# A four-layer gated transformer on one core: placing side work inside two attention streams and a feed-forward block

## Chip, cores and metric

The kernel runs on one core of one Trainium2 chip. The metric is device time in microseconds (us) of one launch. Times are given as the median of three runs; one further execution was recorded by the hardware profiler.

## What is computed

Input `x` is (4, 256, 256), the context is (4, 256, 64). Four layers follow one another, each of the form "x plus tanh(gate) times an attention of the normalised x, then x plus tanh(gate) times a feed-forward of the normalised x". Cut to what the change touches:

```python
# layer 1: attention with 32 query and 8 key heads, then a block with its own causal attention
x = x + tanh(g[1]) * grouped_attention(layernorm(x), ctx, ctx)      # "l1x"
attn = causal_attention(rmsnorm(h), Wq, Wk, Wv) @ Wo.T              # "l1f", h = layernorm(x)
mod = 0.1 * tanh(attn @ A)
gate = silu(h2 @ W_in.T + mod * (h2 @ A) @ B); out = h + gate * (h2 @ W_up.T) @ W_down.T
# layer 2: adjacency from two score vectors, then a block with quantised rows and ternary weights
x = x + tanh(g[2]) * (0.6 * sigmoid(si + sj + b) + 0.4 * layernorm(x))
h = layer_norm(gelu(silu(bitlinear(layernorm(x), w1, b1))), ln_g, ln_b)
x = x + tanh(f[2]) * bitlinear(h, w2, b2)
#   bitlinear: scale = 127 / max|row|; q = clip(round(row * scale)) / scale; q @ ternary(w).T + b
# layer 3: grouped attention, then a soft mixture of 16 experts with 128 slots each
x = x + tanh(g[3]) * (grouped_attention(layernorm(x), ctx, ctx) @ Wc.T + bc)   # "l3x"
mu_n = mu / max(sqrt(sum(mu * mu, axis=0)), 1e-12)                  # the slot norms
logits = einsum(l2norm(x_ln), mu_n); ...
```

## The kernel before

The program is one static stream of instructions for each engine; nothing is scheduled by a planner. The order is written by hand, as Python loops with conditions on a pair (slot, tile), and semaphores link the engines. The token rows stay in on-chip memory the whole time (`xs`, tiles of 128 rows by 256). Every batch has two such tiles.

In order of time the stages are:

- up to about 474 us: preparation of weights, layer 0's attention and its mixture of experts;
- 474 to 768 us: the first attention stream, called "A" in the code, which holds layer 1's two attentions for all four batches;
- 768 to 935 us: layer 1's feed-forward in two halves of 512 tokens, layer 2's adjacency, and the first half of layer 2's quantised block;
- 935 to 1105 us: the second attention stream, "C", which is layer 3's attention, with the quantised block's second half in between;
- from there on: the soft mixture.

**A stream.** `attention(stream)` loops over slots `sl`, from -3, and over tiles `k` from 0 to 7. A slot is one group of heads of one batch. Stream A has 16 slots of l1x (four to a batch, so batch 0 has slots 0 to 3, and `LAST["l1x", b]` is 3, 7, 11, 15), then 8 of l1f. Stream C has 8 slots of l3x, two to a batch. At tile k TensorE makes scores for slot `sl` with the keys as rows (`by_key`, L1064, read by ScalarE's exponential) and for slot `sl + 2` with the queries as rows (`by_query`, L1016, of which VectorE takes the largest value, L2120). GpSimd splits these maxima into bf16 parts, a DMA lays them out again, and TensorE turns them (`turn_maxima`, L1027). Queries and keys of slot `sl + 3` are turned at tiles 3, 5, 6 and 7 (L948, L969), `weighted` (L1084) multiplies with the values, and once in each slot `rows_again` (L1100, rows of `otr`) turns an output back into rows.

**The batch's way from l1x to l1f** lies between these steps. When the last l1x slot of batch b, slot e, is through, VectorE adds and normalises the rows (`between`), GpSimd applies weights (`rows_in`), and TensorE turns the two results (`turn_rows`, L611 on `tmp` and `qr`), then projects to queries and keys (`queries_and_keys`, L1117, two steps for each of two halves) and values (`values`). All the turnings and these projections, and rows_again, share two banks of the product memory, `left0` and `left1`, in an order that `bank_uses` sorts from the same (slot, tile) pairs; a step can take its bank once the step two places before it has been copied out by ScalarE or VectorE. Before, TensorE does `turn_rows` at (e+2, 6) and (e+2, 7), the first projections at (e+3, 0) and (e+3, 1), the second ones at (e+3, 5) and for batches 0 and 1 (e+3, 6), the values at (e+4, 0) and (e+4, 1).

**The slot norms.** `slot_products` (L1280) sums the squares of `mu` by 64 products of one column, VectorE takes the reciprocal roots (`slot_norms`, 19 operations on 128x16), `turn_slot_parts` turns them, `spread_slots` spreads them over partitions into banks 6 and 7, and VectorE scales `mu` (`scale_slots`). They stand in the first half of the feed-forward, between its gate groups (`gate_and_up`, L1253 and L1255).

**The quantised block**, half h. ScalarE normalises and centres (L1702, L1709), quantises, and TensorE multiplies (`l2_up`). ScalarE makes silu and gelu, VectorE the layer norm (`l2_shift`, L2372) and the largest value of each row (L2375). `l2_square` (L1736) sums squares on ScalarE. VectorE then scales and rounds the hidden rows in one pass, by adding and later subtracting a large constant (`l2_round_hidden`, L2384), ScalarE makes bf16 of them (`l2_second_quantised`, L1742), TensorE turns and multiplies (`l2_last`: `turn_hidden` L1337, `l2_down` L1346), VectorE adds the rows (L2393) and takes their statistics. For h = 1, `l2_last` stands at (-1, 7) of stream C, ahead of slot 0. The third banks of both halves are in `L2_BANKS`. ScalarE's `norm` (L1570) and GpSimd's parts of the queries and keys (L2575, L2578) of batches 2 and 3 need these rows.

The two loops on which the order in TensorE's stream hangs:

```python
for sl in range(-3, S_ + (1 if stream == "A" else 2)):
    for k in range(8):
        if inside(sl) and k < tiles_of(groups[sl][0]):
            by_key(sl, k)
...
        if inside(sl + 2) and k < tiles_of(groups[sl + 2][0]):
            by_query(sl + 2, k)
```

## Time and profile before

| what | value |
|---|---|
| runs | 1325.32, 1324.08, 1322.42 us; median 1324.08 |
| profiled execution | 1326.74 us |
| its span, first to last instruction | 1325.0 us |
| granted clock of TensorE, mean | 0.916 of full |
| TensorE, matrix products (PE) | 1057.4 us busy, 80% |
| TensorE, weight loads (PEld) | 672.3 us |
| VectorE (DVE) | 740.0 us, 56% |
| ScalarE (ACT) | 525.4 us, 40% |
| GpSimd (POOL) | 328.2 us, 25% |

"Busy" is time in which an engine runs an instruction. In a row of the timeline, the first number is the start in us, the second the duration, the bracket the idle time before it and the instruction that ended the wait. `L1100` is a line of the kernel. A name with q, such as DVEq, is the engine's own queue, a semaphore instruction without work. The rows quoted in a later section are of this one execution.

### The profile page before, as it was taken

The numbers are of one execution on the slowest core, as the hardware profiler recorded it, in microseconds if no ns is written. First come the engines' busy times: TensorE is split into PE (matmuls) and PEld (weight loads), VectorE is DVE, ScalarE is ACT, GpSimd is POOL, SyncE is SP. The second block draws the span as 40 slices with busy tenths as digits, with TensorE's granted clock in tenths as the row PEclk, the third lists the DMA queues.
The fourth block names the chain that finished last, engine by engine and source line by source line (L and its number), as shares of the span: only waits on it lengthen the run. The fifth ranks groups of instructions, "written<-read, shape, count | busy, mean of one in ns | idle before, by whom it ended". The sixth has DMA issues, their size and how long they took to land.

```text
span 1325.0 us, 19053 instructions
## 1 busy us (share of the span) xinstructions
PE 1057.4 (80%) x6622; PEld 672.3 (51%) x6625; DVE 740.0 (56%) x1684; ACT 525.4 (40%) x883; POOL 328.2 (25%) x626
## 2 busy tenths in 40 slices
PE   4245999999999678778798889984252888899997
PEld 2124888888888533233355645533232443475565
DVE  3654444544454646685655512457777765676644
...
DMA packets 62441, 32.06 MB, mean 24 GB/s; under 512 B 47104, under 2 KB 61072, under 8 KB 62112
## 3 DMA queue, kind: packets, MB, share of 16 engines
...
q14 instruction: 29, 0.24, 0.1%
...
## 4 chain that ended last, share of the span: by engine, by line
PE 69%; DVE 20%; ACT 4%; issue 4%; POOL 1%; SPq 0%; DMA 0%; POOLq 0%; DVEq 0%; ACTq 0%; PEldq 0%
PE bank L692 15%; PE bank L708 7%; PE bank L800 4%; PE bank L1084 3%; DVE mx L2120 3%; PE bank L915 2%; PE bank L883 2%; PE bank L1016 2%; PE bank L1270 2%; PE bank L845 2%; PE bank L1253 2%; PE bank L1064 2%; PE bank L1255 2%; PE bank L1117 2%; PE bank L1100 1%
## 5 line engine op out<-in xcount | busy, mean ns | idle before, releaser
L2120 DVE TENSOR_REDUCE mx<-bank 128x2 f32<-128x512 f32 (+1 forms) x176 | 118.1, 689 | 88.6 <-PE bank L1016 44.8
L1594 ACT ACTIVATE prob<-bank 128x512 f32<-128x512 f32 x176 | 102.7, 597 | 100.1 <-PE bank L1064 78.3
L1433 ACT ACTIVATE hhi<-hh 128x512 fp32r<-128x512 f32 x72 | 45.5, 632 | 153.1 <-DVE hh L1957 140.5
L1953 DVE TENSOR_TENSOR hu<-bank,sg 128x512 f32<-128x512 f32 x64 | 44.3, 692 | 101.6 <-PE bank L692 101.6
L692 PE MATMUL bank<-xh,wh 128*128 128x512 f32 x288 | 91.5, 398 | 0.7 <-POOL wl L2539 0.7
L692 PE MATMUL bank<-xh,wl 128*128 128x512 f32 x288 | 90.5, 395 | 0.0
L692 PE MATMUL bank<-xlo,wh 128*128 128x512 f32 x288 | 90.1, 394 | 0.0
L1945 DVE TENSOR_TENSOR hlo<-hh,hhi 128x512 fp32r<-128x512 f32 x72 | 57.1, 793 | 50.6 <-ACT hhi L1433 50.6
L2539 POOL TENSOR_TENSOR wl<-wraw,wh 128x512 fp32r<-128x512 f32 x72 | 80.4, 1117 | 13.0 <-POOL wh L2536 13.0
L1472 ACT ACTIVATE sg<-bank 128x512 f32<-128x512 f32 x72 | 43.1, 598 | 64.8 <-PE bank L692 64.8
L692 PEld LDWEIGHTS bank<-xh,wh 128*128 128x128 f32 x288 | 54.4, 189 | 14.6 <-POOL wl L2539 1.6
L692 PEld LDWEIGHTS bank<-xlo,wh 128*128 128x128 f32 x288 | 54.3, 189 | 13.4
L692 PEld LDWEIGHTS bank<-xh,wl 128*128 128x128 f32 x288 | 54.4, 189 | 12.4
L800 PE MATMUL bank<-mun,xT 128*128 128x512 f32 x128 | 59.2, 607 | 1.2 <-ACT xw L1433 1.1
L708 PE MATMUL bank<-hhi,wh 128*128 128x512 f32 x144 | 56.8, 394 | 0.9 <-DVE hlo L1945 0.9
L708 PE MATMUL bank<-hhi,wl 128*128 128x512 f32 x144 | 56.9, 395 | 0.0
L708 PE MATMUL bank<-hlo,wh 128*128 128x512 f32 x144 | 56.1, 390 | 0.0
L1016 PE MATMUL bank<-kTx,qT 48*128 48x256 bf16 x256 | 51.4, 308 | 3.7 <-DVE kTx L2084 3.1
L1064 PE MATMUL bank<-qT,kTx 51*128 51x512 bf16 x128 | 51.9, 421 | 2.6 <-ACT prob L1594 2.5
L2120 DVE TENSOR_REDUCE mxc<-bank 128x2 f32<-128x512 f32 x64 | 42.6, 687 | 20.2 <-PE bank L1016 19.1
L1594 ACT ACTIVATE probc<-bank 128x512 f32<-128x512 f32 x64 | 37.5, 596 | 40.0 <-PE bank L1064 39.4
L1337 PE MATMUL bank<-identb,q 128*128 128x128 bf16 x64 | 7.8, 298 | 56.7 <-ACT q L1742 56.7
...
## 6 DMA issues: line engine op xcount, KB each, us to landing
...
```

Source lines behind the costliest of these rows:

```text
L692: last = mm(bank[4 + (n + m) % 4][:, :], w[k % 2][:, m, cc * P:(cc + 1) * P], v[:, cc, tok], start=j == 0 and cc == 0, stop=j == 2 and cc ...
L708: last = mm(bank[2 * m + h][:, :], w[k % 2][:, 2, m * P:(m + 1) * P], v[h][:, :], start=False, stop=last_pair and j == 2, skip_group_check ...
L800: last = mm(bank[n % 2][:, :], xT3[b % 2][:, cc, i * P:(i + 1) * P], mun[:, cc, ch * 512:(ch + 1) * 512], start=cc == 0, stop=cc == 1)
L1016: last = mm(to[:, f * N:(f + 1) * N], t.qT[rows, s % 4, u, i * P:(i + 1) * P], key_operand(L, b, s, 8 * g + 2 * j + f, rows, slice(0, N)), ...
L1064: last = mm(to[:, :], key_operand(L, b, s, 8 * g + 2 * j, rows, slice(ti * P, (ti + 1) * P)), t.qT[rows, s % 4, u:u + 2, :], start=True, s ...
L1433: return act.activation(dst, src, ACT.Copy, scale=scale)
L1472: act.activation(sg[k % 2][:, :], bank[4 + n % 4][:, :], ACT.Silu).then_inc(once("gate_used"), 1)
L1594: act.activation(t.prob[k][:, :], bank[3 + n % 2][:, :], ACT.Exp).then_inc(S("probs"), 1)
L1945: tt(hlo[k % 2][:, :], hh[k % 2][:, :], hhi[k % 2][:, :].bitcast(F32), ALU.subtract)\
L1953: tt(hu[k % 2][:, :], bank[4 + (n + 1) % 4][:, :], sg[k % 2][:, :], ALU.mult).then_inc(once("up_used"), 1)
L2120: V.reduce_max(out_, bank[n % 3][:, :].rearrange("p (h t) -> p h t", h=heads), AX, negate=True)\
L2539: G.tensor_tensor(low[:, cols, :], wraw[k][:, cols, :], high[:, cols, :].bitcast(F32), ALU.subtract)\
```

## The change

Four things are placed differently.

1. *First stream.* A table `BETWEEN` now gives the places of the turnings and projections. For batches 0 and 1 the turnings go from (e+2, 6) and (e+2, 7) to (e+3, 0) and (e+3, 1), the first projections from (e+3, 0) and (e+3, 1) to (e+3, 5) and (e+3, 6), the second ones to (e+4, 0) and (e+4, 1), the values to (e+4, 5) and (e+4, 6). For batch 2 the projections go to (e+4, 0/1) and (e+5, 0/1), the values to (e+6, 0/1). Batch 3 is as it was. The copies on ScalarE and VectorE that empty the banks move with them, as `_out` says.
2. *Slot norms.* They leave the first half of the feed-forward and stand in the second, from its gate group 1 on; all four spreads use bank 7. The turned parts' copy on ScalarE moves along.
3. *Rounding pass.* ScalarE does it as an Identity with scale and bias (`l2_round_hidden`), before each tile's quantising, for both halves. VectorE only signals that the scales are ready.
4. *Last products of the second half.* `l2_last(1)` and all that feeds it from the squares on move from (-1, 7) to (0, 7) of stream C, on banks 0 to 2, and ScalarE's norms of batches 2 and 3 to (1, 0) and (2, 0).

```diff
@@ -49,6 +49,28 @@
+Between = namedtuple("Between", "t0 t0_out t1 t1_out qk0 qk0_out qk1 qk1_out v v_out")
+
+
+def between_at(b):
+
+    e = LAST["l1x", b]
+    if b == B - 1:
+        return Between(t0=(e + 2, 6), t0_out=(e + 2, 7), t1=(e + 2, 7), t1_out=(e + 3, 0), qk0=((e + 3, 0), (e + 3, 1)),
+                       qk0_out=(e + 3, 1), qk1=((e + 3, 5), (e + 3, 5)), qk1_out=(e + 3, 5), v=((e + 4, 0), (e + 4, 1)),
+                       v_out=(e + 4, 1))
+    if b == B - 2:
+        return Between(t0=(e + 3, 0), t0_out=(e + 3, 1), t1=(e + 3, 1), t1_out=(e + 3, 2), qk0=((e + 4, 0), (e + 4, 1)),
+                       qk0_out=(e + 4, 1), qk1=((e + 5, 0), (e + 5, 1)), qk1_out=(e + 5, 2), v=((e + 6, 0), (e + 6, 1)),
+                       v_out=(e + 6, 1))
+    return Between(t0=(e + 3, 0), t0_out=(e + 3, 1), t1=(e + 3, 1), t1_out=(e + 3, 2), qk0=((e + 3, 5), (e + 3, 6)),
+                   qk0_out=(e + 3, 7), qk1=((e + 4, 0), (e + 4, 1)), qk1_out=(e + 4, 2), v=((e + 4, 5), (e + 4, 6)),
+                   v_out=(e + 4, 7))
+
+
+BETWEEN = [between_at(b) for b in range(B)]
@@ -74,9 +96,9 @@
-            e = LAST["l1x", b]
-            at += [(e + 2, 6, 4, ("t", b, 0)), (e + 2, 7, 4, ("t", b, 1)), (e + 3, 0, 4, ("qk", b, 0)),
-                   (e + 3, 5, 4, ("qk", b, 1)), (e + 4, 0, 4, ("v", b))]
+            w = BETWEEN[b]
+            at += [(*w.t0, 4, ("t", b, 0)), (*w.t1, 4, ("t", b, 1)), (*w.qk0[0], 4, ("qk", b, 0)),
+                   (*w.qk1[0], 4, ("qk", b, 1)), (*w.v[0], 4, ("v", b))]
...
+L2_LATE_BANKS = ((4, 5, 6), (0, 1, 2))
...
-            b = L2_BANKS[h][n % 3]
+            b = (L2_BANKS if n < Q2T_USE[0] else L2_LATE_BANKS)[h][n % 3]
...
@@ -991,6 +1014,8 @@
+                    if stream == "C" and n == 24:
+                        pe.wait_ge(S("l2_rows"), 2 * T0)
...
@@ -1033,7 +1058,7 @@
                     if stream == "C" and n == 0:
-                        pe.wait_ge(S("l2_rows"), 2 * T0)
+                        pe.wait_ge(S("l2_pre"), 16)
...
@@ -1170,21 +1195,20 @@
                             if stream == "A":
-                                e = LAST["l1x", b]
-                                if (sl, k) == (e + 2, 6):
+                                w = BETWEEN[b]
+                                if (sl, k) == w.t0:
                                     turn_rows(b, 0)
-                                if (sl, k) == (e + 2, 7):
+                                if (sl, k) == w.t1:
                                     turn_rows(b, 1)
-                                if sl == e + 3 and k < 2:
-                                    queries_and_keys(b, 0, k)
-                                if (sl, k) == (e + 3, 5):
-                                    queries_and_keys(b, 1, 0)
-                                    if b >= 2:
-                                        queries_and_keys(b, 1, 1)
-                                if (sl, k) == (e + 3, 6) and b < 2:
-                                    queries_and_keys(b, 1, 1)
-                                if sl == e + 4 and k < 2:
-                                    values(b, k)
+                                for cc in range(DC):
+                                    if (sl, k) == w.qk0[cc]:
+                                        queries_and_keys(b, 0, cc)
+                                for cc in range(DC):
+                                    if (sl, k) == w.qk1[cc]:
+                                        queries_and_keys(b, 1, cc)
+                                for i in range(NT):
+                                    if (sl, k) == w.v[i]:
+                                        values(b, i)
                             else:
                                 e = LAST["l3x", b]
...
                                     l2_up(1, i)
-                            if (sl, k) == (-1, 7):
+                            if (sl, k) == (0, 7):
...
-                if ch >= 2:
-                    pe.wait_ge(S("mu_normed"), ch - 1)
+                else:
+                    pe.wait_ge(S("mu_normed"), ch)
-                    last = mm(bank[6 + ch % 2][:, e % 4 * SS:(e % 4 + 1) * SS], sel[:, e, :], cmT[:, :], start=True, stop=True)
+                    last = mm(bank[7][:, e % 4 * SS:(e % 4 + 1) * SS], sel[:, e, :], cmT[:, :], start=True, stop=True)
-                if n >= 3:
+                if h == 1 and Q2T_USE[0] <= n < Q2T_USE[0] + 3:
+                    pe.wait_ge(S("maxed"), 24)
+                elif n >= 3:
-                    pe.wait_ge(S("mu_normed"), 4)
+                    pe.wait_ge(S("cT2"), 2)
...
@@ -1360,34 +1386,31 @@
 
             for f in range(F1 // P):
                 gate_and_up(0, f)
-                if f == 1:
-                    slot_products()
-                if f == 3:
-                    turn_slot_parts()
-                if f == 5:
-                    spread_slots(0)
-                    spread_slots(1)
-                if f == 6:
-                    spread_slots(2)
-                if f == 7:
-                    spread_slots(3)
             gate_and_up(1, 0)
             for i in range(T0):
                 down(0, i)
             for f in range(1, F1 // P):
                 gate_and_up(1, f)
+                if f == 1:
+                    slot_products()
                 if f == 4:
                     turn_inputs(0)
                 if f == 5:
+                    turn_slot_parts()
                     l2_up(0, 0)
                     l2_up(0, 1)
                 if f == 6:
+                    spread_slots(0)
                     l2_up(0, 2)
                     l2_up(0, 3)
+            spread_slots(1)
             for i in range(T0):
                 down(1, i)
+                if i < 2:
+                    spread_slots(2 + i)
             l2_last(0)
             pe.wait_ge(S("ffn_out"), 2 * T0)
+            pe.wait_ge(S("mu_normed"), 4)
 
             attention("C")
...
@@ -1613,10 +1636,9 @@
-                        if stream == "C" and k == 0 and inside(sl + 4) and groups[sl + 4][1] >= 2 and groups[sl + 4][2] == 0:
-                            if groups[sl + 4][1] == 2:
-                                act.wait_ge(S("ln_x"), 2)
-                            norm(groups[sl + 4][1])
+                        if stream == "C" and (sl, k) in ((1, 0), (2, 0)):
+                            act.wait_ge(S("ln_x"), 2)
+                            norm(sl + 1)
...
@@ -1651,10 +1673,11 @@
                             if (sl, k) == (-2, 6):
                                 for i in range(T0):
                                     l2_gelu(1, i)
-                            if (sl, k) == (-1, 7):
+                            if (sl, k) == (0, 7):
                                 for i in range(T0):
                                     l2_square(1, i)
                                 for i in range(T0):
+                                    l2_round_hidden(1, i)
                                     l2_second_quantised(1, i)
                                 for i in range(T0):
...
+            def l2_round_hidden(h, i):
+
+                act.wait_ge(S("l2_r2"), h + 1)
+                act.activation(h2[:, i, :], h2[:, i, :], ACT.Identity, bias=l2v[:, 57:58], scale=l2v[:, 52 + i:53 + i])\
+                    .then_inc(S("l2_r3"), 1)
+
-                act.wait_ge(S("l2_r2"), T0 * h + i + 1)
+                act.wait_ge(S("l2_r3"), T0 * h + i + 1)
...
-                if f == 4:
-                    act.wait_ge(S("mu_partsT_ps"), 1)
-                    copy(cmT[:, :], bankb[7][0:96, 0:P]).then_inc(S("mu_partsT"), 1)
+            act.wait_ge(S("mu_partsT_ps"), 1)
+            copy(cmT[:, :], bankb[7][0:96, 0:P]).then_inc(S("mu_partsT"), 1)
...
@@ -2226,6 +2255,7 @@
                                     l2_stats(1, i)
                                 l2_norm2(1)
                                 l2_shift(1)
+                            if (sl, k) == (0, 7):
                                 l2_round_hidden(1)
                                 l2_add(1)
                                 stats_of(step, 0.25, range(T0, 2 * T0))
...
-                for i in tiles:
-                    ts(h2[:, i, :], h2[:, i, :], l2v[:, 52 + i:53 + i], ROUND, ALU.mult, ALU.add).then_inc(S("l2_r2"), 1)
+                dve.sem_inc(S("l2_r2"), 1)
...
@@ -2396,16 +2425,11 @@
 
             for f in range(F1 // P):
                 hidden(0, f)
-                if f == 2:
-                    slot_norms()
                 if f == 4:
                     l2_scores(0)
                     l2_scores(1)
-                if f >= 5:
-                    scale_slots(f - 5)
             dve.wait_ge(once("late_rows"), len(rowsF) * 16)
             hidden(1, 0)
-            scale_slots(3)
             for i in tiles:
                 add_down(0, i)
             l2_norm(0)
@@ -2415,19 +2439,24 @@
             l2_round_inputs(0)
             hidden(1, 3)
             hidden(1, 4)
+            slot_norms()
             l2_pre(0, 0)
             l2_pre(0, 1)
             hidden(1, 5)
             l2_pre(0, 2)
             l2_pre(0, 3)
             hidden(1, 6)
+            scale_slots(0)
             hidden(1, 7)
+            scale_slots(1)
             l2_stats(0, 0)
             l2_stats(0, 1)
             add_down(1, 0)
+            scale_slots(2)
             l2_stats(0, 2)
             l2_stats(0, 3)
             add_down(1, 1)
+            scale_slots(3)
             l2_norm2(0)
```

The first place is TensorE's order in slots 5 and 6 of stream A, for batch 0 (e = 3). `kstx` is a key operand, `tmp` and `qr` are the two results to be turned, `wqkvT` the projection's weights. Before:

```order
L969 MATMUL bank<-identb,kstx 128x128 x8
L1016 MATMUL bank<-kTx,qT 128x256 x2
L1064 MATMUL bank<-qT,kTx 128x512
L611 MATMUL bank<-ident,tmp 128x128 x4
L1016 MATMUL bank<-kTx,qT 128x256 x2
L1064 MATMUL bank<-qT,kTx 128x512
L969 MATMUL bank<-identb,kstx 128x128 x8
L611 MATMUL bank<-ident,qr 128x128 x4
L1016 MATMUL bank<-kTx,qT 128x256 x2
L1064 MATMUL bank<-qT,kTx 128x512
L1117 MATMUL bank<-wqkvT,xT 128x512
```

and after the change:

```order
L992 MATMUL bank<-identb,kstx 128x128 x8
L1041 MATMUL bank<-kTx,qT 128x256 x2
L1089 MATMUL bank<-qT,kTx 128x512
L1041 MATMUL bank<-kTx,qT 128x256 x2
L1089 MATMUL bank<-qT,kTx 128x512
L992 MATMUL bank<-identb,kstx 128x128 x8
L1041 MATMUL bank<-kTx,qT 128x256 x2
L1089 MATMUL bank<-qT,kTx 128x512
L634 MATMUL bank<-ident,tmp 128x128 x4
```

with the second turning behind it, after the products with the values:

```order
L1109 MATMUL bank<-prob_173,vstx 32x512
L634 MATMUL bank<-ident,qr 128x128 x4
L1041 MATMUL bank<-kTx,qT 128x256 x2
L1089 MATMUL bank<-qT,kTx 128x512
```

The turnings of `tmp` and `qr` no longer stand ahead of the second key turning and right behind it, but after it and in the next slot; the two projection steps, formerly behind the second turning (the first of them is the last row of the first piece), follow at that slot's tiles 5 and 6.

The second place is ScalarE's order around the second half's squares (`q_225,l2v<-h_224`, and `h_224` is the hidden rows). Before, at the end of the slots ahead of slot 0 (`probc` are the exponentials of slot 0):

```order
L1433 ACTIVATE qTc<-bank 96x1024
L1736 ACTIVATE q_225,l2v<-h_224 128x1024 x4
L1742 ACTIVATE q_225<-h_224,l2v 128x1024 x4
L1433 ACTIVATE q2T<-bank 128x8x128 x4
L1594 ACT_TABLE_LOAD
L1594 ACTIVATE probc_197<-bank 128x512
L1570 ACTIVATE xnc<-xs,nmx,rsx 128x256 x2
L1594 ACTIVATE probc_198<-bank 128x512
L1594 ACTIVATE probc_199<-bank 128x512
L1594 ACTIVATE probc_200<-bank 128x512
L1433 ACTIVATE mTc<-bank 24x256
```

and after the change, where slot 0's exponentials come first:

```order
L1617 ACTIVATE probc_200<-bank 128x512
L1456 ACTIVATE mTc<-bank 24x256
L1617 ACTIVATE probc_201<-bank 128x512
L1456 ACTIVATE qTc<-bank 96x1024
L1617 ACTIVATE probc_202<-bank 128x512
L1617 ACTIVATE probc_203<-bank 128x512
L1617 ACTIVATE probc_204<-bank 128x512
L1759 ACTIVATE q_225,l2v<-h_224 128x1024 x4
L1764 ACTIVATE h_224<-h_224,l2v 128x1024
L1771 ACTIVATE q_225<-h_224,l2v 128x1024
L1764 ACTIVATE h_224<-h_224,l2v 128x1024
L1771 ACTIVATE q_225<-h_224,l2v 128x1024
```

The squares now stand behind slot 0's eight exponentials, and each quantising is preceded by a rounding of the same rows.

## Rows read from the trace of the kernel before

**Rows 1.** Busy time by stage: us, PE, PEld, DVE, ACT, POOL (instructions), PEclk, DMA share, GB/s
```profile
474.00:768.00 294.00, 238.32 (x2448) 118.57 (x2448) 182.38 (x410) 155.88 (x275) 115.88 (x309) 0.87 0.01 4
...
935.00:1105.00 170.00, 99.14 (x993) 54.19 (x994) 122.40 (x290) 87.06 (x134) 31.56 (x81) 0.75 0.01 2
```

**Rows 2.** Timeline, TensorE, slots 5 and 6: start, us, instruction [idle before <-releaser]
```profile
544.01 0.63 PE L611 MATMUL bank<-ident,tmp 128*128 128x128 f32 x4 [2.23 <-DVEq L2143]
...
546.99 1.03 PE L969 MATMUL bank<-identb,kstx 128*128 128x128 bf16 x8 [2.02 <-DVE kTx L2084]
...
550.89 2.04 PE L1117 MATMUL bank<-wqkvT,xT 128*128 128x512 f32 x2 [1.47 <-DVE kTx L2084]
...
561.50 1.12 PE L1117 MATMUL bank<-wqkvT,xT 128*128 128x512 f32 x2
```

**Rows 3.** Timeline, TensorE: the output turnings of slots 5 to 8
```profile
538.95 0.63 PE L1100 MATMUL bank<-ident,otr 128*128 128x128 f32 x4 [0.18 <-ACT mT L1433]
...
559.62 0.63 PE L1100 MATMUL bank<-ident,otr 128*128 128x128 f32 x4 [0.73 <-ACT mT L1433]
...
570.65 0.66 PE L1100 MATMUL bank<-ident,otr 128*128 128x128 f32 x4
...
577.97 0.63 PE L1100 MATMUL bank<-ident,otr 128*128 128x128 f32 x4 [0.18 <-ACT mT L1433]
```

**Rows 4.** Timeline, TensorE: the output turnings of slots 13 to 16
```profile
634.86 0.67 PE L1100 MATMUL bank<-ident,otr 128*128 128x128 f32 x4 [0.18 <-ACT mT L1433]
...
660.18 0.66 PE L1100 MATMUL bank<-ident,otr 128*128 128x128 f32 x4
...
677.83 0.66 PE L1100 MATMUL bank<-ident,otr 128*128 128x128 f32 x4
...
688.35 0.61 PE L1100 MATMUL bank<-ident,otr 128*128 128x128 f32 x4
```

**Rows 5.** Timeline, TensorE, the feed-forward block
```profile
787.10 1.98 PE L1253 MATMUL bank<-hT,winT 128*128 128x512 f32 x4
...
791.78 10.23 PE L1280 MATMUL bank<-ones,mu 128*128 128x1 f32 x64
...
869.36 3.78 PE L1253 MATMUL bank<-hT,winT 128*128 128x512 f32 x4 [3.16 <-DVE gu L2265]
```

**Rows 6.** Timeline, ScalarE and VectorE, the quantised block's first half
```profile
917.86 2.08 ACT L1702 ACTIVATE xn<-xs,l2v 128x256 f32<-128x256 f32 x4 [17.45 <-DVEq L2311]
...
935.39 2.74 DVE L2384 TENSOR_SCALAR h<-h,l2v 128x1024 f32<-128x1024 f32 x4
...
941.75 1.70 ACT L1709 ACTIVATE xn<-xs,l2v 128x256 f32<-128x256 f32 x4 [1.30 <-DVEq L2324]
```

**Rows 7.** Timeline, ScalarE and VectorE, the second half's last chain
```profile
1000.85 1.06 ACT L1736 ACTIVATE q<-h 128x1024 bf16<-128x1024 f32 x1 [18.43 <-DVE h L2372]
...
1004.43 4.42 DVE L2375 TENSOR_REDUCE l2v<-h 128x4 f32<-128x4096 f32 x1
...
1013.01 4.27 ACT L1742 ACTIVATE q<-h,l2v 128x1024 bf16<-128x1024 f32 x4 [7.42 <-DVE h L2384]
...
1024.59 0.48 DVE L2393 SCALAR_TENSOR_TENSOR xs<-bank,l2v,xs 128x256 f32<-128x256 f32 x1 [0.81 <-PE bank L1346]
```

**Rows 8.** Timeline, from the norm to the turning of slot 2's maxima
```profile
1029.59 1.09 ACT L1570 ACTIVATE xnc<-xs,nmx,rsx 128x256 f32<-128x256 f32 x2 [3.44 <-DVEq L2232]
...
1030.82 0.40 POOL L2575 CAST qstc<-xnc 128x256 bf16<-128x256 f32 x1 [43.46 <-ACT xnc L1570]
...
1031.22 0.61 PE L1064 MATMUL bank<-qTc,kTc 99*128 99x512 bf16 x1 [4.09 <-ACT probc L1594]
...
1034.57 0.43 POOL L2578 TENSOR_TENSOR kstc<-leftc,kstc 128x128 bf16<-128x128 f32 x1
...
1038.46 0.20 POOL L2646 CAST mstc<-mxc 128x16 bf16<-128x16 f32 x1 [3.47 <-DVE mxc L2120]
...
1039.84 0.28 PE L1027 MATMUL bank<-identb,mstc 128*24 128x128 bf16 x2
```

22 lines of the change are left out of this document (11 added, 11 removed), and 1 row of the table STAGES.

## Prediction

> **What bounds the kernel now.** I read the granted clock and the busy time by stage first, then the order of TensorE's waits in the first attention stream, then the chain through the quantised block. In the first stream (474 to 768 us) TensorE is busy 238 of 294 us, at 0.87 of its full clock; in the second stream with the quantised block's second half (935 to 1105 us) 99 of 170 us, at 0.75 [rows 1]. TensorE is the bound, with holes; every term below is a hole that closes, moves or opens. I call one turn of the slot loop a slot; the marks for a slot's length are the four turnings back of an output (`rows_again`), one set in each slot.
>
> **The first stream, batches 0 and 1.** In slot 5 TensorE waits 2.23 us for the first turning's input, 2.02 us at the key turning and 1.47 us before the first projection, 5.7 us in all; after that two projection steps take 2.04 us where the same two take 1.12 us later [rows 2]. A quiet slot takes 7.3 us (570.65 to 577.97), the two disturbed ones 31.7 us together (538.95 to 570.65) [rows 3]. Two quiet slots and the moved work (two turnings at 0.63, six projection groups at about 1.12: 7.9 us) make 22.5; 9.2 us are loss.
>
> The key turning waits for VectorE's copy of the keys before it, and VectorE doesn't get there sooner when TensorE does. So the first two waits (4.3 us) become one wait of about 4.3 us at the key turning, before which the turning of `tmp` no longer fits: it costs 0.6 us that was hidden. What goes is the third wait (1.5) and the double price of the projections (1.8, twice 2.04 less 1.12), since they now stand in the middle of slot 6, after TensorE has worked again. 1.5 + 1.8 - 0.6 = 2.7 us for batch 0, the same for batch 1, whose stretch repeats it. Bounds: 0.9 (the clock stays low as long as before) and 4.9 (of the 9.2 only the 4.3 stay).
>
> **Batch 2** meets the masked attention's slots. Slots 13 to 15 take 25.3 and 17.65 us between marks, the next 10.5 us [rows 4]; 43.0 less two such slots (21.0) less the work (7.9) is 14.1 us of loss. The wait for the key copy with its slow stretch stays (about 5 us by batch 0's rows), and I add 1.6 us for two buffers that are now taken while their copy is under way (a wait of the kind of 0.7 to 0.9 us at the mark of slot 6 [rows 3]). 14.1 - 5.0 - 1.6 = 7.5 us. The values, moved to slot 17, run beside VectorE's next chain of small operations and cost TensorE nothing; without that cover they'd cost 2.2. Bounds: 3 (waits reappear at each moved step) and 9. Batch 3 stays in place.
>
> **The slot norms.** The 64 one-column products take 10.2 us [rows 5] in either place, and so do the turning and the four spreads. They leave the first half of the feed-forward and come back in the second, behind the group that stands before VectorE's two norms. There TensorE waits 3.16 us for VectorE and then runs four products in 3.78 us that otherwise take 1.98 [rows 5]. With 10.2 us of work put in front, VectorE is ready before TensorE asks: 3.2 + 1.8 = 5.0 us gained. The small operations on VectorE move into its waits between gate groups, which are 4.7 us apart (787.10 to 791.78 [rows 5]); uncovered they'd cost up to 4. Bounds: 3 and 6.
>
> **The rounding pass, first half.** It leaves VectorE (four tiles in 2.74 us, 0.69 each) and goes to ScalarE, where the quantising that follows takes 4.27 us for four [rows 6, 7]. It has a scale operand more; four such of 256 columns take 2.08 against 1.70 us, 0.1 us each [rows 6]. So a rounding is 1.17, a pair 2.24, four pairs about 9.0 us, strictly one after the other. ScalarE starts when VectorE's scales are there (935.4), ends at 944.4, then centres the other half (1.7 us): 946.1 instead of 943.4, so 2.7 us lost. Bounds 2.2 and 3.3.
> The Trainium skill speaks against this move (VectorE: DVE Perf Modes, the perf-mode tier table: a float32 tensor_scalar within SBUF runs at two results a cycle; ScalarE: Activation LUTs, What ACT_TABLE_LOAD costs: one element a cycle whatever the function, 280 ns and 0.833 ns per column with a pointer bias, 93 ns for each further pointer). The trace agrees in kind, 0.69 against 1.07 us. By the page's figures, as an estimate, a pair is 2.36 us, and the sum below would be 0.8 us worse over both halves.
>
> **The last products of the second half** move behind slot 0 of the second stream. I count from the end of VectorE's largest-value reduction (1004.43 + 4.42 = 1008.85 [rows 7]) to the turning of slot 2's maxima (1039.84 [rows 8]): 31.0 us now. Then, in series:
> - rest of slot 0 (tiles 3 to 7), since its third tile waits for VectorE's maxima: 7.0. A whole turn of eight tiles, from 1031.22 to 1039.84, takes 8.6 [rows 8]: ceiling that, floor five eighths of it, 5.4; the middle, since TensorE has idled before.
> - the four squares, until now beside VectorE, but placed behind the slot's exponentials: 4 x 1.2 = 4.8 (1.06 and the read of the sum [rows 7]).
> - VectorE's scales: 1013.01 - 1008.85 - 0.7 = 3.4 [rows 7].
> - four pairs on ScalarE: 9.0.
> - copies, turnings, products and the row additions: 1025.07 - 1017.3 = 7.8 [rows 7].
> - statistics of the new rows: 1029.59 - 1025.07 = 4.5 [rows 7, 8].
> - ScalarE's norm: 1.1 [rows 8].
> - GpSimd, whose order is unchanged: the query and key parts of batch 2 (1030.82 to 1035.00) 4.2, and only behind them slot 2's maxima (1038.46 to 1039.84) 1.4 [rows 8]. Before, those parts were ready 3.5 us ahead of the maxima.
>
> With 0.2 between them that is 43.4 us, 12.4 more. While GpSimd works TensorE waits some 8 us, and before (4.09 us [rows 8]) it ran at the lower level for a few us after such a wait; I add 1.0. Total 13.4 lost, bounds 10 and 18. What comes back for it, TensorE's slot 0 beside VectorE's normalisation, is in this count already: only its first three tiles.
>
> **Sum:** -2.7 - 2.7 - 7.5 - 5.0 + 2.7 + 13.4 = -1.8 us. The profiled execution took 1326.74 us (span 1325.0); the median of the runs is 1324.08, 2.7 below it. Taken off the median: **1322.3 us**. About 2.6 us (0.2%) is what a measurement can tell from no change, so this is a small gain or none.
>
> **The rivals.**
> 1. *The balance tips to slower: VectorE's backlog keeps the first stream.* Place: the key turning at the end of slots 5, 9 and 13. If the moved turnings find VectorE still behind, each later take of the two turning buffers waits for a copy, and the lower clock lasts as before. For it: TensorE's waits there name VectorE's key copy. Against it: VectorE has caught up by the third wait. The three batches then give 0.9 + 0.9 + 3.0 in place of 12.9: +6.3, 1330 us. It decides from a gain under 8.5 us in the first stream. Chance 0.22.
> 2. *The clock stays high.* If the spread work keeps TensorE fuller, the slow stretches (3.5 us of the 9.2 for each of batches 0 and 1, as much for batch 2) go as well, and batch 0 and 1 give 4.9 each, batch 2 9: with the quantised block at its lower bound (10 and 2.2) the sum is -11.6, 1312.5 us; with the block as counted -7.7, 1316. The Trainium skill (TensorE: Matmul & The Clock Gate, the part on the HAM clock gate) says that the throttled state is the default and activity releases it; that is this rival's rule. Against it: 4.3 us of idle stays. Chance 0.24.
> 3. *The quantised block's chain is longer than counted* (its second wait reaches the transfers of the maxima and the slots after): 18 in place of 13.4 and 3.3 for 2.7: +3.4, 1327.5. Chance 0.10.
> 4. *The late products don't hold the second stream* (GpSimd's parts fit, as before, in front of the maxima): 5 us less, -6.8, 1317. Chance 0.06.
>
> **How the numbers follow.** My forecast, the sum within about 3.5 us (1318.8 to 1325.8), has 0.38. Of it 0.26 lies within 0.2% and 0.12 below. Slower: rival 1 whole (0.22) and most of rival 3 (0.08). Faster: 0.12, rival 2 (0.24) and rival 4 (0.05). That makes 0.41 faster, 0.29 same, 0.30 slower. The range takes rivals 1 and 2: 1313 to 1331; in it are all cases but the outer ends of both.
>
> **What would show it.** In the new profile: marks of slots 5 to 7 some 3 us closer, of slots 13 to 15 some 7 closer or more, with one wait of about 4 us at the key turning; no wait of 3 us before the fourth gate group of the second half; eight ScalarE passes over the hidden rows in about 9 us, twice; TensorE idle for about 8 us ahead of the turning of slot 2's maxima, with GpSimd as the releaser. The prediction is wrong if the second stream reaches that turning less than 9 us late against the end of the reduction, or if the first stream shortens by less than 8 or more than 17 us.

## The result, and the profile after

The changed kernel takes 1333.22 us, median of five runs (1331.97 to 1338.64), against 1324.32 us of the kernel before, also of five (1322.42 to 1330.24). The ratio is 1.0068, with a 95% interval of 1.004 to 1.0096: 5 to 13 us slower. The forecast was 1322.3 us in a range of 1313 to 1331. Sign and range are both missed.

The profiled execution took 1331.97 us. From its page:

```profile
span 1330.2 us, 19059 instructions
## 1 busy us (share of the span) xinstructions
PE 1058.5 (80%) x6625; PEld 672.2 (51%) x6625; DVE 733.1 (55%) x1677; ACT 534.9 (40%) x891; POOL 329.0 (25%) x626
```

The same stretches of time as in [rows 1], start and end, length, PE, PEld, DVE, ACT, POOL (instructions), granted clock, DMA share, GB/s:

```profile
474.00:768.00 294.00, 242.43 (x2473) 120.79 (x2472) 184.57 (x432) 157.80 (x279) 118.59 (x305) 0.89 0.04 15
...
935.00:1105.00 170.00, 98.67 (x957) 51.00 (x955) 107.20 (x241) 84.11 (x128) 31.65 (x81) 0.74 0.01 2
```

The stages are no longer in the same places, so I cut both profiles at marks instead: the first and last output turning of the first stream (line 1100 before, 1125 after), the end of the feed-forward's last down product, the start of the quantised block's last product of the first half, the last turning of maxima in the second stream, and the end. The runs of the experiments are cut at the same marks in the tables further down. All are us of one profiled execution for each kernel.

| profile | first stream | feed-forward | first half | second stream | rest |
|---|---|---|---|---|---|
| before | 263.9 | 142.9 | 40.7 | 142.2 | 232.1 |
| changed | 256.6 | 136.9 | 43.6 | 158.7 | 233.0 |
| difference | -7.2 | -6.0 | +3.0 | +16.5 | +0.9 |
| forecast | -12.9 | -5.0 | +2.7 | +13.4 | 0 |

The differences make +7.1; the profiled execution of the change also began 1.9 us sooner ahead of these stages, where nothing was changed. Against the forecast's -1.8, the first stream is 5.7 us short, the second 3.1 too long, the first half 0.3 and the rest 0.9; the feed-forward gives back 1.0. The two profiled executions are only 5.2 us apart and the medians 8.9, so 3.7 us of the loss are not in this table; the runs of single parts below come closer to it.

**First stream, batch 0.** TensorE's timeline of the changed kernel in slots 5 to 8 (start, duration, instruction, idle before it and its releaser):

```profile
537.08 0.63 PE L1125 MATMUL bank<-ident,otr 128*128 128x128 f32 x4 [0.18 <-ACT mT L1456]
...
542.06 0.62 PE L992 MATMUL bank<-identb,kstx 128*128 128x128 bf16 x8 [1.83 <-DVEq L2172]
...
545.21 1.09 PE L634 MATMUL bank<-ident,tmp 128*128 128x128 f32 x4 [2.21 <-DVE kTx L2113]
548.03 0.37 PE L1041 MATMUL bank<-kTx,qT 48*128 48x256 bf16 x1 [1.73 <-DVE kTx L2113]
...
553.66 0.61 PE L971 MATMUL bank<-identb,qst 128*128 128x128 bf16 x8 [1.25 <-ACT hT L1456]
...
554.53 0.66 PE L1125 MATMUL bank<-ident,otr 128*128 128x128 f32 x4
...
556.44 1.12 PE L1142 MATMUL bank<-wqkvT,xT 128*128 128x512 f32 x2
...
565.32 0.61 PE L971 MATMUL bank<-identb,qst 128*128 128x128 bf16 x8 [1.53 <-DVE qkf L2113]
...
566.18 0.66 PE L1125 MATMUL bank<-ident,otr 128*128 128x128 f32 x4
...
575.38 0.63 PE L1125 MATMUL bank<-ident,otr 128*128 128x128 f32 x4 [0.41 <-ACT mT L1456]
...
585.08 1.11 PE L1125 MATMUL bank<-ident,otr 128*128 128x128 f32 x4
```

The marks of slots 5 and 9 are 48.0 us apart (585.08 less 537.08), and so were those of the kernel before (586.96, from the same view, less 538.95 [rows 3]). The kernel before waited three times in slot 5, 2.23, 2.02 and 1.47 us, 5.7 in all [rows 2]. The changed one waits three times too, 1.83, 2.21 and 1.73 us, 5.8 in all, for the same three things: VectorE's work on the slot's output, its copy of the first keys and its copy of the second keys. Only the step that waits is another: the third wait stood ahead of the projection and now stands ahead of a scores product (`kTx,qT`), which needs the same copy. VectorE's two key copies, before and then changed:

```profile
546.26 0.68 DVE L2084 COPY kTx<-bank 128x1024 bf16<-128x1024 bf16 x1
...
550.06 0.68 DVE L2084 COPY kTx<-bank 128x1024 bf16<-128x1024 bf16 x1
```

```profile
544.39 0.68 DVE L2113 COPY kTx<-bank 128x1024 bf16<-128x1024 bf16 x1
...
547.10 0.68 DVE L2113 COPY kTx<-bank 128x1024 bf16<-128x1024 bf16 x1
```

Counted from the mark of slot 5 the first copy starts at 7.3 us in both, the second at 11.1 before and 10.0 after. On top of that, two old steps (the next query turnings) now wait 1.25 and 1.53 us, because a moved step holds the turning buffer (releasers `hT` and `qkf`, the copies of the moved steps); before, this stretch had two waits of 0.73 and 0.93 us (the second from the same view). The projections are at 1.12 us as forecast, but the turning of `tmp` takes 1.09 in place of 0.63. So slot 5 shortens by 3.2 us, and 0.6, 1.9 and 0.7 come back in slots 6, 7 and 8. Slot 7 holds the two value steps now (2.2 us of work that slot 6 had before), but slot 6 didn't get shorter for their leaving: the 2.6 us by which slots 5 and 6 shorten together are little more than this work. At the end of slot 8 TensorE is at its lower level (1.11 us for a turning of an output, 0.63 at a quiet mark).

**Batch 2.** The marks of slots 13, 14, 15 and 18:

```profile
632.59 1.11 PE L1125 MATMUL bank<-ident,otr 128*128 128x128 f32 x4
...
651.24 0.66 PE L1125 MATMUL bank<-ident,otr 128*128 128x128 f32 x4
...
664.17 0.66 PE L1125 MATMUL bank<-ident,otr 128*128 128x128 f32 x4
...
707.72 0.61 PE L1125 MATMUL bank<-ident,otr 128*128 128x128 f32 x4
```

From 632.59 to 707.72 are 75.1 us, before 634.86 to 716.88, 82.0 us (the first mark stands in [rows 4], the last is from the same view): 6.9 gained. In the ten profiles with batch 2's new places this stretch takes 75.0 to 75.3 us, in the five with all old places 82.0 to 82.1.

**The feed-forward.** Behind the one-column products, before and then changed, with the changed kernel's gate group 4 of the second half (counted from 0) at the end:

```profile
801.87 3.76 PE L1253 MATMUL bank<-hT,winT 128*128 128x512 f32 x4
```

```profile
833.93 9.95 PE L1304 MATMUL bank<-ones,mu 128*128 128x1 f32 x64
843.73 3.76 PE L1277 MATMUL bank<-hT,winT 128*128 128x512 f32 x4
...
855.41 1.98 PE L1277 MATMUL bank<-hT,winT 128*128 128x512 f32 x4
```

No gate group waits any more, and group 4, which took 3.78 us behind its wait [rows 5], takes 1.98. The 3.76 us behind the one-column products stood there before the change too and moved along with them.

**The second half's chain**, ScalarE, VectorE, GpSimd and TensorE:

```profile
992.27 4.42 DVE L2405 TENSOR_REDUCE l2v<-h 128x4 f32<-128x4096 f32 x1
...
1008.10 0.17 DVE L2410 TENSOR_SCALAR ve<-l2v 128x4 f32<-128x4 f32 x1 [3.11 <-ACT q L1759]
...
1003.82 1.05 ACT L1759 ACTIVATE q<-h 128x1024 bf16<-128x1024 f32 x1
...
1011.48 1.24 ACT L1764 ACTIVATE h<-h,l2v 128x1024 f32<-128x1024 f32 x1 [3.41 <-DVEq L2413]
1012.75 1.15 ACT L1771 ACTIVATE q<-h,l2v 128x1024 bf16<-128x1024 f32 x1
...
1019.68 1.15 ACT L1771 ACTIVATE q<-h,l2v 128x1024 bf16<-128x1024 f32 x1
...
1033.81 1.09 ACT L1593 ACTIVATE xnc<-xs,nmx,rsx 128x256 f32<-128x256 f32 x2 [4.19 <-DVEq L2262]
...
1035.04 0.40 POOL L2604 CAST qstc<-xnc 128x256 bf16<-128x256 f32 x1 [59.83 <-ACT xnc L1593]
...
1039.46 0.20 POOL L2675 CAST mstc<-mxc 128x16 bf16<-128x16 f32 x1 [0.23 <-POOL kstc L2607]
...
997.47 0.61 PE L1041 MATMUL bank<-kTc,qTc 96*128 96x256 bf16 x2 [20.78 <-DVE mxc L2149]
...
1040.61 0.39 PE L1052 MATMUL bank<-identb,mstc 128*24 128x128 bf16 x2 [9.04 <-POOLq L2679]
1040.93 0.61 PE L1041 MATMUL bank<-kTc,qTc 96*128 96x256 bf16 x2
...
1051.65 0.28 PE L1052 MATMUL bank<-identb,mstc 128*24 128x128 bf16 x2
```

TensorE waits 20.8 us for VectorE's normalisation, runs the rest of slot 0, waits for the pairs on ScalarE, and waits 9.04 us more ahead of the turning of slot 2's maxima (1040.61).

### The profile page after: what moved, and what is told of

Read it like the earlier page. It is cut to its first block, busy times and chain, and to the rows that moved or that the text cites. A ratio compares the mean times of both kernels' runs of the same rounds, so it can differ in the third digit from the quotient of the medians.

```text
span 1330.2 us, 19059 instructions
## 1 busy us (share of the span) xinstructions
PE 1058.5 (80%) x6625; PEld 672.2 (51%) x6625; DVE 733.1 (55%) x1677; ACT 534.9 (40%) x891; POOL 329.0 (25%) x626
## 4 chain that ended last, share of the span: by engine, by line
PE 69%; DVE 19%; ACT 5%; issue 4%; POOL 1%; SPq 0%; DMA 0%; POOLq 0%; DVEq 0%; ACTq 0%; PEldq 0%
PE bank L715 15%; PE bank L731 7%; PE bank L823 4%; PE bank L1109 3%; DVE mx L2149 3%; PE bank L938 2%; PE bank L1277 2%; PE bank L1041 2%; PE bank L906 2%; PE bank L1294 2%; PE bank L868 2%; PE bank L1279 2%; PE bank L1089 2%; PE bank L1142 1%; PE bank L922 1%
## 5 line engine op out<-in xcount | busy, mean ns | idle before, releaser
L715 PEld LDWEIGHTS bank<-xlo,wh 128*128 128x128 f32 x288 | 54.3, 189 | 13.4
L715 PEld LDWEIGHTS bank<-xh,wl 128*128 128x128 f32 x288 | 54.4, 189 | 12.4
L2565 POOL CAST wh<-wraw 128x512 fp32r<-128x512 f32 x72 | 37.7, 523 | 58.8 <-PE bank L715 30.1
```

The costliest lines, as they stand in the source:

```text
L715: last = mm(bank[4 + (n + m) % 4][:, :], w[k % 2][:, m, cc * P:(cc + 1) * P], v[:, cc, tok], start=j == 0 and cc == 0, stop=j == 2 and cc ...
```

## The experiments

Each kernel is compared with the kernel before on the same chip, as a ratio with a 95% interval. The runs were made in four groups on three chips, so I compare kernels of different groups by these ratios, not by their medians. A time in us that I give for a ratio is the ratio times 1325.

**One part alone.** Each kernel is the one before with one of the four parts of the diff, otherwise unchanged. Where the rounding stays on VectorE, `l2_round_hidden` is the loop of `ts(...)` over four tiles as before; where the late products stay, `l2_last(1)` and what feeds it stand at (-1, 7).

> The kernel before, with only the first stream's new table of places. Theory A (the parts add as the two profiles show them: the stretch from the first output turning to the last gets 7.2 us shorter, none of it from batches 0 and 1, 6.8 from batch 2): 7 us faster than before, about 1317; marks of slots 5 to 9 as far apart as before (48 us). Theory B (the prediction's terms were right, and something else in the whole change took the gain of batches 0 and 1 away): 12.9 us faster, slots 5 to 9 in about 45 us.

> The kernel before, with only the slot norms in the feed-forward's second half. Theory A: the 3.2 us wait of TensorE before the fourth gate group of the second half and part of the slow matrix products behind it go, 5 to 6 us faster (1318 to 1319). Theory B (the gain was borrowed from another moved part, as the earlier arrival at the feed-forward): 2 us or less.

> The kernel before, with only the rounding pass on ScalarE, in both halves, the last products where they were. Theory A: 2.8 us lost in the first half (read from the two profiles) and 5.0 in the second, where nothing stands between the pairs and the turnings: 7 to 8 us slower (about 1332). Theory B (a pair on ScalarE overlaps VectorE's work): 5.4 or less, 2.7 a half as predicted.

> The kernel before, with only the last products of the second half moved behind slot 0 of the second stream, rounding still on VectorE. Theory A (chain through squares, scales, products, statistics and GpSimd's parts stands in series behind slot 0): 10 to 12 us slower (1334 to 1336), with TensorE idle for about 9 us ahead of the turning of slot 2's maxima. Theory B (the late place costs only with the rounding on ScalarE): within 4 us of before.

| run | median us | ratio | interval | first stream | feed-forward | first half | second stream |
|---|---|---|---|---|---|---|---|
| stream only | 1321.78 | 0.9968 | 0.9949 to 0.9988 | 257.4 | 143.1 | 40.7 | 145.1 |
| norms only | 1319.76 | 0.9951 | 0.9932 to 0.9969 | 264.0 | 136.9 | 40.3 | 144.6 |
| rounding only | 1334.27 | 1.007 | 1.0045 to 1.0095 | 264.0 | 142.9 | 43.7 | 148.7 |
| late products only | 1333.89 | 1.0079 | 1.0049 to 1.0109 | 260.0 | 142.9 | 40.7 | 153.7 |

By the ratios that is -4.2, -6.5, +9.3 and +10.5 us: +9.1 together, the change as measured is +9.0. The stream and the norms gain, the rounding pass and the late products each lose more than either gain. Each of these four carries 2.5 to 4 us of uncertainty to either side. Against the forecast (-12.9, -5.0, and by its terms +6.6 for the rounding and +9.5 for the late products) the first stream misses by 8.7 us, more than the other three together. I had expected 7 us of gain for the stream and 7 to 8 us of loss for the rounding. (In the rounding run the view merges the last two products of the first half into one row; the mark is the start of the last one, 952.10.)

The rounding pass costs 3.0 us in the first half and 6.5 in the second stream. Its profile in the second half, ScalarE:

```profile
1013.84 1.24 ACT L1767 ACTIVATE h<-h,l2v 128x1024 f32<-128x1024 f32 x1 [6.69 <-DVEq L2416]
...
1022.05 1.15 ACT L1774 ACTIVATE q<-h,l2v 128x1024 bf16<-128x1024 f32 x1
1023.10 1.92 ACT L1458 ACTIVATE q2T<-bank 128x1024 bf16<-128x1024 bf16 x2
```

The four pairs take 9.3 us here, against 5.1 for VectorE's four passes with ScalarE one behind (1012.22, where the first pass starts, to 1017.28 [rows 7]). Then the copies of the turned rows stand behind all four pairs on ScalarE (1023.10), and TensorE stays longer at its lower level in the turnings and products that follow (granted clock 0.65 between 1024 and 1032 us, against 0.78 between 1018 and 1025 before): from the first pair (1013.84) to TensorE's next product of slot 0 (1032.21 in the same view) are 18.4 us, before, from 1012.22 to 1025.13, 12.9.

The table shows something else. The second stream takes 142.2 us before, and 145.1 and 144.6 where only earlier stages were changed; the first stream 260.0 us where it wasn't touched at all (late products only). That led to the next question.

**Parts put together, and batches apart.** The stream and the norms together; batches 0 and 1 alone; batch 2 with the norms. In the table of places the batches left out got back the tuple that stands for the old code:

```diff
+    if b in (2,):
+        return Between(t0=(e + 2, 6), t0_out=(e + 2, 7), t1=(e + 2, 7), t1_out=(e + 3, 0), qk0=((e + 3, 0), (e + 3, 1)),
+                       qk0_out=(e + 3, 1), qk1=((e + 3, 5), (e + 3, 6 if b < 2 else 5)), qk1_out=..., v=((e + 4, 0), (e + 4, 1)), ...)
```

> The changed kernel with its rounding pass back on VectorE and its last products back ahead of slot 0, so the first stream's table and the slot norms alone. Theory A (the two gains of the single runs, 4 and 6 us, stand beside one another, since one closes before the other begins): 10 to 11 us faster than before, about 1315. Theory B (the earlier start of each later stage is eaten by longer stretches of the lower clock in the second stream, where each single run took 2 to 3 us more than before): 8 us or less in the profile, with the last turning of maxima over 144 us after the first half's last product.

> The kernel before with the new places for batches 0 and 1 only. Theory A (VectorE's copies are late by the same amount wherever the turnings stand, and the waits only move to them): no change beyond the noise; marks of slots 5 to 9 and of 9 to 13 as far apart as before, 48.0 and 47.9 us within 0.5. Theory B (the profile of the whole change hid a gain that its later marks lost to another batch): 5.4 us faster, 45 us for each four slots.

> Batch 2's new places and the slot norms; batches 0 and 1 as before. Theory A (batches 0 and 1 lose about what their own run lost, 7 us, whatever stands around them): 7 us faster than the stream and the norms together, about 1309. Theory B (batches 0 and 1 change nothing by themselves; what their own run lost is stretches at the lower clock that come with the time of arrival, so losses of single parts don't add): as fast as the stream and the norms together within 2 us, about 1315; slots 5 to 9 and 9 to 13 in 48 us each as before, slots 13 to 18 in some 59 in place of 63.7.

| run | median us | ratio | interval | first stream | feed-forward | second stream |
|---|---|---|---|---|---|---|
| stream and norms | 1315.89 | 0.9918 | 0.9896 to 0.9939 | 260.1 | 140.2 | 144.6 |
| batches 0 and 1 only | 1333.75 | 1.0061 | 1.0038 to 1.0084 | 266.8 | 146.4 | 142.4 |
| batch 2 and norms | 1314.15 | 0.9926 | 0.9905 to 0.9947 | 253.5 | 140.1 | 142.7 |

Batches 0 and 1 alone make the kernel 8 us slower, where I had expected no change, and yet taking them out of "stream and norms" gains nothing that the intervals can tell: theory B of the third run. Batch 2 and the norms gain 3.3 us more than the norms alone, give or take some 4. In the run of batches 0 and 1 the marks of slots 5, 9 and 13 are 48.0 and 47.5 us apart, as far as before, so its profile shows no loss where the moved steps stand. It is further on, in steps that were not moved: slots 13 to 17, 66.3 us in place of 63.7, behind the same waits of 2.52, 1.62 and 1.46 us (66.3 again in the second profile with these places, shown below), and the entry of the feed-forward block. At this entry TensorE waits 2.52 us in both kernels. In the one before, the turnings behind it and the next products:

```profile
770.33 1.97 PE L1224 MATMUL bank<-ident,at_f 128*128 128x128 f32 x16 [2.52 <-POOLq L481]
772.23 3.61 PE L1229 MATMUL bank<-hT,am 128*16 128x512 f32 x8
```

and with batches 0 and 1 moved:

```profile
771.53 3.68 PE L1249 MATMUL bank<-ident,at_f 128*128 128x128 f32 x16 [2.52 <-POOLq L507]
775.14 4.50 PE L1254 MATMUL bank<-hT,am 128*16 128x512 f32 x8
```

The same wait, the same instructions, 1.97 and 3.61 us against 3.68 and 4.50: TensorE ran them at its lower level (granted clock 0.66 of full between 770 and 780 us, and 1.00 in the profile before). The profiled execution as a whole is 5.1 us longer than that of the kernel before; what makes the rest of the 8 us stays open. Fifteen of the seventeen profiles have this wait unfilled, 2.51 or 2.52 us long: in twelve the turnings take 1.97 us, in three 2.37 to 3.68. There is one profile for each kernel, so they can't tell whether the edit decides this or the single execution. With the old places of batch 0 its four slots took 45.4 to 48.0 us in seven profiles, with the new ones 48.0 to 52.2 in ten, so the new places of batch 0 gain nothing and on the whole cost something. Batch 1's four slots took 47.6 to 48.0 us with the old places and 47.5 to 48.3 with the new ones.

**The lower level tested by filling waits.** If TensorE has products to do in the wait, no level should be lost. The first wait tried is the one at the entry of the feed-forward:

```diff
             attention("A")
+            keep_clock(6, 10)
             pe.wait_ge(S("at_done"), 2 * B)
```

`keep_clock(k, n)` is a helper of the kernel: n products of 128x512 into bank k, whose values nobody reads.

> The run with batch 2's places and the norms, with ten more matrix products (128x512, bf16, into a bank that is free) in TensorE's wait of 2.5 us at the entry of the feed-forward block. Theory A (what the wait costs beyond itself is the lower clock behind it, which some runs show and others don't): the sixteen turnings behind the wait take 2.0 us in each profile, and the median falls by 0 to 2.5 us. Theory B (the clock has nothing to do with the wait): the products cost their own time, up to 2 us slower.

> The run with the new places of batches 0 and 1 only, with ten more matrix products (128x512, bf16, into a bank that is free) in TensorE's wait of 2.5 us at the entry of the feed-forward block. Theory A (2.6 of the 7 us that run lost are the lower clock at that entry): 2 to 3 us faster than that run, about 1331, with the sixteen turnings there in 2.0 us in place of 3.7. Theory B (the loss sits elsewhere): 1333 to 1334.

Measured: with batch 2 and the norms 1313.52 us (0.9917, 0.9896 to 0.9937), against 1314.15 (0.9926) without; with batches 0 and 1 alone 1331.22 us (1.0043, 1.0029 to 1.0057), against 1333.75 (1.0061) on another chip. The entry of the latter:

```profile
772.06 2.10 PE L652 MATMUL bank<-mask_q,identb 128*128 128x512 bf16 x9 [1.24 <-DVEq L2176]
774.00 1.91 PE L1249 MATMUL bank<-ident,at_f 128*128 128x128 f32 x16
775.84 3.61 PE L1254 MATMUL bank<-hT,am 128*16 128x512 f32 x8
```

The turnings take 1.91 us and the products 3.61, and so they do in the other filled kernel. The filling products start 1.24 us into the wait and end 0.7 us after it would have ended, so from the last output turning to the first gate group are 15.9 us, against 17.9 unfilled and 15.3 in the kernel before: 2.0 us back. That the filling did it isn't shown: twelve of fifteen unfilled profiles have the upper level there too, and the ratios differ by 1.2 and 2.4 us, with intervals that overlap.

The other wait is the one of 9.04 us in the late arrangement. The products go into the bank that the turning writes next:

```diff
+                    if stream == "C" and s == 2:
+                        r, full, _ = of_use(stream, ("m", s))
+                        pe.wait_ge(S(f"left{r % 2}"), r // 2)
+                        for _ in range(24):
+                            mm(full[:, :], identb[:, :], mask_q[:, :, :], start=True, stop=True, skip_group_check=True)
                     pe.wait_ge(S("max_parts"), s + 1)
```

> The changed kernel, with 24 more matrix products (128x512, bf16, into the bank that the turning is about to write) in TensorE's wait of 9.0 us ahead of the turning of slot 2's maxima. Theory A (3.2 us of the late products' loss over the prediction is the lower clock behind that wait): slot 2's to slot 3's turning of maxima takes 8.8 us in place of 11.0; 2 to 4 us faster than the change, about 1330. Theory B (these slots are longer for their new order of work): still 11.0 us between the two turnings, no change in the median or some tenths slower.

> The changed kernel, with 44 more matrix products (128x512, bf16, 0.22 us each at the full clock, 9.5 in all) in the wait of 9.0 us ahead of the turning of slot 2's maxima. Theory A (the slow slots behind the wait are the lower clock, and the 24 products failed since 3.85 us of idleness were left): 8.8 us from slot 2's to slot 3's turning in place of 11.0, 1 to 2 us faster than the change if the products end with the wait. Theory B (the slots are long by their work): 11.0 us stay, and the products that overrun make it up to 1 us slower.

With 24 products the median is 1333.55 us (1.0077, 1.0054 to 1.0099), with 44 it is 1330.82 (1.0045, 1.0021 to 1.0069); the change itself has 1.0068. TensorE with 24, then with 44:

```profile
1032.65 5.12 PE L1053 MATMUL bank<-mask_q,identb 128*128 128x512 bf16 x23
1041.62 0.39 PE L1057 MATMUL bank<-identb,mstc 128*24 128x128 bf16 x2 [3.85 <-POOLq L2684]
1041.94 0.61 PE L1041 MATMUL bank<-kTc,qTc 96*128 96x256 bf16 x2
...
1052.66 0.28 PE L1057 MATMUL bank<-identb,mstc 128*24 128x128 bf16 x2
```

```profile
1031.30 9.44 PE L1053 MATMUL bank<-mask_q,identb 128*128 128x512 bf16 x43
1040.67 0.28 PE L1057 MATMUL bank<-identb,mstc 128*24 128x128 bf16 x2
...
1049.21 0.28 PE L1057 MATMUL bank<-identb,mstc 128*24 128x128 bf16 x2
```

My own expectation of the first was wrong by a count: 23 recorded products took 5.1 us and left 3.85 idle, and the level fell as if nothing had been done (granted clock 0.50 between 1041 and 1047 us). With 44 the wait is full to its end, the clock stays at 1.00, and from slot 2's turning to slot 3's are 8.5 us in place of 11.0. All four profiles with this wait open or half filled have 11.0 to 11.3 us there. So some 2.3 to 2.5 us of the late products' loss are the lower level, by the profiles. The medians fit, but the intervals of this run and of the change overlap.

Slots 4 to 5 take 18.1 us in the changed kernel, 16.9 in this run and 16.8 before; behind the same wait of 2.45 us at batch 3's keys TensorE is at its lower level in one and not in the others. This is not a price of the late products: the runs with the stream only, the norms only and both have 18.1 us there as well, and the late products alone have 16.8.

**GpSimd's order and the squares.** In the changed kernel GpSimd splits slot 2's maxima before, not after, it waits for the query rows of batch 2:

```diff
-                    if inside(sl + 1):
+                    if inside(sl + 1) and not (stream == "C" and sl == 1):
                         max_parts(sl + 1)
+                    if stream == "C" and sl == 0:
+                        max_parts(2)
```

> The changed kernel with one edit: GpSimd splits slot 2's maxima before it waits for the query parts of batch 2, not after. Theory A (GpSimd's order puts 4.2 us of query and key parts and 1.2 of its own work in front of the turning of slot 2's maxima): the wait of 9.0 us there goes, and one of some 4 us comes at the turning of slot 4's queries instead; 4 to 6 us faster than the change, about 1328. Theory B (the row statistics and the norm bound the stage, whatever GpSimd does first): within 1.5 us of the change.

> The run with only the last products moved, with two edits: ScalarE's squares stay ahead of slot 0's exponentials, where VectorE's normalisation covers them, and GpSimd splits slot 2's maxima first. Theory A (the chain counted in series: squares 4.3 us, GpSimd 4.4 us of the 11.5 us lost): 8 to 9 us faster than the last products alone, 2 to 3 us slower than before, about 1328. Theory B (slot 0's exponentials, now behind the squares, hold TensorE instead): no faster than 1331.

With the maxima first the change takes 1326.75 us (1.0021, 1.0003 to 1.004), 6 us less by the ratios. The long wait is gone and two shorter ones stand for it:

```profile
1036.94 0.39 PE L1089 MATMUL bank<-qTc,kTc 99*128 99x512 bf16 x1 [3.33 <-ACT probc L1617]
1039.00 1.04 PE L978 MATMUL bank<-identb,qstc 128*32 128x128 bf16 x24 [1.67 <-POOLq L2655]
```

With both edits, and the rounding on VectorE, the late products take 1328.78 us (1.0012, 0.9992 to 1.0032), 9 us less than the late products alone, and within the noise of the kernel before. So GpSimd's order was a cost on the path by the first run, and GpSimd's order and the squares together were 9 us by the second; the squares had no run of their own. No gain is left even then. My reading is that the chain through the rows of batch 2 keeps its length wherever the products stand, and that slot 0 is all that can go beside it; no run tests this.

**The change less one part.**

> The changed kernel with its rounding pass back on VectorE, in both halves. Theory A (the pass costs the same in any surrounding, 2.4 us in the first half and 5 in the second by the profile of its own run): 7 to 9 us faster than the change, about 1325. Theory B (the late place hides part of it behind TensorE's slots, so the two losses overlap): 3 to 5 us faster, about 1329.

> The changed kernel with its last products back ahead of slot 0. Theory A (parts add: stream and norms 10 us faster than before, rounding on ScalarE 9 slower): 1325, level with before, 8 us faster than the change. Theory B (the losses overlap): 3 to 5 us faster than the change, about 1329.

The change without the rounding on ScalarE: 1325.94 us (0.9998, 0.9975 to 1.0021), 9 us less than the change by the ratios. Without the late products: 1322.72 us (0.9992, 0.997 to 1.0014), 10 us less. So both losses are found inside the change at about the size that they have alone, give or take 5 us. The profiles are finer and show a part that overlaps: from the end of VectorE's largest-value reduction to the turning of slot 2's maxima are 31.0 us before, 37.2 with the rounding alone, 40.0 with the late products alone and 43.9 with both. Next to the late products the rounding adds 3.9 us to this chain, alone 6.2.

**What beats both kernels:** best are the stream and the norms, or batch 2 and the norms, with or without the filled entry: 1313.5 to 1315.9 us, 0.7 to 0.8% faster than before. Among the three the intervals decide nothing. The norms alone (0.5%) and the stream alone (0.3%) are faster than before too.

## Why the prediction was wrong, point by point

The step that failed first is the gain of the first stream: forecast -12.9 us, measured -4.2 by the ratio of its own run and -7.2 in the profile of the change. By the single runs 8.7 of the some 11 us between the forecast (-1.8) and the result (+9.0) are there. The rest are prices that were too low, 2.7 us for the rounding and 1.0 for the late products, less 1.5 that the norms gave beyond their term.

- *What bounds the kernel.* TensorE with holes: right. Left out was that a hole has two prices, its length and the level behind it, and that the second is not fixed.
- *Batches 0 and 1, -2.7 each.* Wrong: 0.0 and -0.4 in the marks of the change, no more than that in the nine other profiles with these places, and 8 us lost by the ratio where they are moved alone. The step that failed is "what goes is the third wait". That wait is for VectorE's copy of the second keys. The projection no longer stands behind it, but the next scores product does (1.73 us for 1.47), so it stayed; the three waits make 5.8 us where they made 5.7. Two more came (1.25 and 1.53 us), since the moved steps take the two turning buffers in turn with the old ones. I had priced such waits only for batch 2. "VectorE doesn't get there sooner" was right for the first key copy and should have been carried through to the second; rival 1 said it, for all three batches. The double price of the projections went as forecast, and the turning of `tmp` (1.09 for 0.63) and the slots behind took it back. That VectorE's copies hold the stretch is read from the traces; no run made them come earlier.
- *The sign "marks of slots 5 to 7 some 3 us closer"* came (2.6) and was no gain: the two value steps, 2.2 us of work, had left these slots for slot 7. Forecast was one wait of about 4 us at the key turning; there are three of about 2. The sign of being wrong, a first stream shorter by less than 8 us, did come.
- *Batch 2, -7.5.* Near in the marks: -6.9 in the change, and some 7 in every profile with these places. The ratios give less, 3.3 us next to the norms with some 4 to either side, so the size on the whole kernel is open. That the values cost nothing beside VectorE's chain is half right: the slot in which they now stand, 16 to 17, is 2.7 us longer, and only 1.8 come back in slots 17 to 18.
- *Slot norms, -5.0.* Right: -6.0 in the profile, -6.5 alone. The wait and the slow stretch behind it went.
- *Rounding, first half, +2.7.* Right: +3.0, a pair in 2.31 us where I had 2.24. The Trainium skill's figures (ScalarE: Activation LUTs, What ACT_TABLE_LOAD costs) had given 2.36 as an estimate; the measured pair lies between the two. Its rule that spoke against this move (VectorE: DVE Perf Modes, the perf-mode tier table) agrees with this trace: 0.69 us for a rounding on VectorE, 1.22 to 1.24 on ScalarE.
- *Rounding, second half.* Hidden inside the count of the late products, as pairs of 9.0 us against a present 5.1, so +3.9. Inside the change that is what the chain shows (43.9 against 40.0 us). In its own run it is 6.2 on the chain and 6.5 on the second stream, since ScalarE's copies wait for all pairs and TensorE stays longer at the lower level. In the change the term after it ("copies, turnings, products and the row additions", 7.8) grew to 8.5. I never wrote down what this one edit costs in both halves: 6.6 by my terms, 9.3 measured. Without it the change is level with the kernel before.
- *Late products, +13.4 with the second half's rounding in it.* The chain was counted well: 31.0 + 12.4 = 43.4 us, measured 1040.61 less 996.69, 43.9. Its members, measured and then forecast in brackets: rest of slot 0 7.1 (7.0), squares 4.3 (4.8), scales 3.4 (3.4), pairs 9.35 (9.0), products 8.5 (7.8), statistics 4.5 (4.5). TensorE was idle 9.04 us with GpSimd as the releaser, where I had some 8. What was too small is the price of the idleness, 1.0 for the level behind that wait where 2.3 to 2.5 were measured. The second stream came out at +16.5; 1.3 of it are the level at batch 3's keys, which kernels without the late products show too.
- *The rivals.* In the first stream the outcome lies at rival 1: 0.0 and -0.4 where rival 1 had 0.9 each, and for batch 2 6.9 in the marks and 3.3 by the ratios for its 3.0. The block lies between my count and rival 3: 15.2 us without those 1.3, and 3.0 in the first half, against 13.4 and 2.7, and 18 and 3.3. I had given each a case of its own and none to the two together, which would have been 8.1 + 5.2 on the sum, 1335.6 us; nothing keeps the two apart, and the range ended at 1331 since I left the pair out. Rival 2, the high clock, didn't come: the granted clock is 0.89 in the first stream where it was 0.87, and 0.74 in the second where it was 0.75. The Trainium skill's rule (TensorE: Matmul & The Clock Gate, the part on the HAM clock gate) is that activity releases the low state. The trace of the run with 44 products agrees, with a granted clock of 1.00 through the wait and behind it. That spreading the work would do the same was this rival's own step, and the change didn't show it.
